# Loops over the image pairs written out with constant waits, no counting step between waits, and the pooled copies ahead of the second norm group's scaling

## The reference, cut to what matters

```python
    x = x + _L0_conv_ref(_gn(x), ...)                 # group norm, then a correlation-driven 7-tap convolution,
                                                      # a 1x5 and a dilated 5x5 depthwise convolution
    t = _to_tokens(x)                                 # 3136 tokens of 64 channels for each image
    t = t + _L1_attn_ref(_ln_t(t), ...)               # linear attention, 16 heads, elu+1 features, cos/sin weights
    t = t + _L1_ffn_ref(_ln_t(t), ...)                # 32 experts: softmax over the tokens, top 8 tokens pooled,
                                                      # two dense layers, results scattered back
    x = _from_tokens(t, x)
```

## Time and profile before

| | |
|---|---|
| median of 3 runs | 3701.57 us (3693.27 to 3703.83) |
| the profiled execution's own time | 3709.65 us |
| its span, first to last instruction | 3707.8 us |
| mean granted TensorE clock | 0.961 |
| instructions in the span | 52162 |
| busy share PE, DVE, ACT, POOL | 86%, 76%, 57%, 41% |

### The profile page before, as it was taken

One profiled execution on the slowest core, in us unless ns is written; L12 is line 12 of the kernel. 1 busy time (PEld: TensorE's weight loads), 2 busy tenths in 40 slices (PEclk: granted clock), 3 DMA queues, 4 the chain that ended last, 5 costly groups with the idle time before them and its releaser, 6 DMA issues.

```text
span 3707.8 us, 52162 instructions
## 1 busy us (share of the span) xinstructions
PE 3197.1 (86%) x16628; PEld 1454.1 (39%) x16628; DVE 2826.8 (76%) x3283; ACT 2119.9 (57%) x2329; POOL 1518.6 (41%) x1078
## 2 busy tenths in 40 slices
PE   3698988988899987989889888998879898898955
PEld 2343335433443334433344334433344333443332
DVE  6887877978778886878778787787878787747843
ACT  1067844777457863678546774468636785445530
POOL 1057611865038631576117651286315762110000
PEclk8799999999999998999989999999999999999977
DMA  1002640045200651026400453006510264104566
GB/s 52 14 4 54 137 110 28 1 104 133 73 19 4 149 131 45 1 48 140 113 28 1 93 131 78 28 1 142 132 47 9 46 140 115 33 0 112 132 166 221
DMA packets 69386, 279.62 MB, mean 75 GB/s; under 512 B 30845, under 2 KB 35485, under 8 KB 64221
## 3 DMA queue, kind: packets, MB, share of 16 engines
q1 hardware_dynamic: 69085, 275.89, 30.6%
HBM read 242.78 MB, written 33.05 MB: 74 GB/s over the span
## 4 chain that ended last, share of the span: by engine, by line
PE 55%; DVE 19%; issue 11%; DMA 7%; ACT 5%; SPq 2%; POOL 1%; DVEq 1%; ACTq 0%; POOLq 0%
PE ps_C L1493 9%; PE ps_D L1560 8%; PE ps_A L1478 5%; PE ps_B L1478 5%; PE ps_D L1493 5%; PE ps_E L1493 5%; DVE region L1132 4%; DMA RB<-r_keep 4%; PE ps_E L1539 4%; DVE region L1123 3%; PE ps_A L1371 3%; DVE arena L948 2%; PE ps_A L1522 2%; DMA r_keep<-RR 2%; PE ps_B L1522 2%
## 5 line engine op out<-in xcount | busy, mean ns | idle before, releaser
L592 POOL TENSOR_TENSOR arena<-arena,UHL 128x896 f32<-128x896 f32 x525 | 1095.2, 2089 | 429.7 <-ACT UHL L724 429.7
L1560 PE MATMUL ps_D<-region,small 128*128 128x448 f32 x1792 | 771.2, 555 | 69.6 <-DVE OS L1159 40.2
L733 ACT ACTIVATE ps_C<-RB 128x896 f32<-128x896 f32 x448 | 410.9, 917 | 308.8 <-DVE region L1132 205.3
L1132 DVE TENSOR_TENSOR region<-region,ps_C 128x896 f32<-128x896 f32 x448 | 484.5, 1081 | 93.1 <-ACT ps_C L733 90.4
L724 ACT ACTIVATE UHL<-arena,W8C 128x896 f32<-128x896 f32 x525 | 542.5, 1033 | 0.0
L570 POOL TENSOR_SCALAR ST<-ST 128x14 f32<-128x14 f32 x64 | 22.5, 352 | 1119.8 <-DVE ST L1003 1118.4
L1560 PEld LDWEIGHTS ps_D<-region,small 128*128 128x128 f32 x1792 | 318.7, 190 | 375.1 <-issue 276.7
L602 POOL TENSOR_TENSOR UA<-region,CS 128x128 f32<-128x128 f32 (+1 forms) x400 | 229.4, 575 | 417.2 <-PE ps_C L1493 368.0
L1493 PE MATMUL ps_C<-region,UA 128*128 128x512 f32 (+1 forms) x800 | 378.3, 595 | 1.9 <-ACT region L658 1.7
L948 DVE SCALAR_TENSOR_TENSOR arena<-arena,W8C 128x448 f32<-128x448 f32 (+1 forms) x243 | 365.1, 1524 | 0.0
L751 ACT ACTIVATE region<-ps_A,NEG 128x1024 f32<-128x1024 f32 (+1 forms) x200 | 222.5, 1113 | 198.4 <-PE ps_A L1478 198.3
(11 more groups left out here) (296 smaller groups left out, 4879.9 us busy)
## 6 DMA issues: line engine op xcount, KB each, us to landing
RB<-r_keep SPq DMA_DIRECT2D x448, 448.0 KB, 5.8
arena<-x SPq DMA_DIRECT2D x8, 1568.0 KB, 7.0
t_keep<-Y SPq DMA_DIRECT2D x7, 1568.0 KB, 5.2
r_keep<-RR SPq DMA_DIRECT2D x448, 7.0 KB, 3.4
w_keep<-region SPq DMA_DIRECT2D x7, 784.0 KB, 5.6
CST<-t_keep SPq DMA_DIRECT2D x2, 1568.0 KB, 10.0
small<-t_keep SPq DMA_DIRECT2D x2, 1568.0 KB, 12.9
plane<-w_keep SPq DMA_DIRECT2D x4, 784.0 KB, 15.8
```

The source lines that it names most:

```text
L592: pool.tensor_tensor(out=X[:, cut], in0=X[:, cut], in1=PRODUCT[m % 3], op=ALU.add).then_inc(pool_taps.sem, 1)
L733: act.activation(here.area(key)[:, :].rearrange("p (c n) -> p c n", c=2)[:, :, 0:PIX], RB[:, cc].rearrange("p (c n) -> p c n", c=2), ACT.C ...
L1132: dve.tensor_tensor(out=q, in0=q, op=ALU.mult, in1=here.area(key)[:, :].rearrange("p (c n) -> p c n", c=2)[:, :, 0:PIX])\
L1560: ins = pe.matmul(here.area(key)[:, 0:PIX], MW[i][:, c, :], Q[s % 3][:, c, :], start=c == 0, stop=c == NCHUNK - 1)
```

## The change

The four loops over the pairs become Python loops, so the body is written out seven times with constants in the waits and addresses (PE, DVE, ACT, POOL and SP each have one). `passed` and its semaphore go, at all of its places. And in DVE's `back` the copies of `pooled` stand ahead of `norm1_scale(pair, 1)`.

```diff
-        def passed(eng):
-
-
-            eng.sem_inc(waits_passed.sem, 1)
-
-
...
                 for s in range(STEPS):
                     sp.wait_ge(*recip_ready.at(pair, s + 1))
-                    passed(sp)
                     for q in range(STRIPS):
...
-            with sp.Fori(0, PAIRS - 1) as pair:
+            for pair in range(PAIRS - 1):
                 pair_of_images(Here("loop", pair))
             pair_of_images(Here("last", PAIRS - 1))
...
                 for w in here.all_emptied([("lg", g) for g in range(NG)]):
                     dve.wait_ge(*w)
-                passed(dve)
                 if here.span == "loop":
                     dve.wait_ge(*pool_taps.at(here.pair + 1, POOL_PIECES))
-                    passed(dve)
...
                 low_part(pair, 0)
-                norm1_scale(pair, 1)
                 if before is not None:
                     pooled(here)
+                norm1_scale(pair, 1)
                 conv_residual(here, pair, 2)
                 conv_residual(here, pair, 3)
...
-            with dve.Fori(0, PAIRS - 1) as pair:
+            for pair in range(PAIRS - 1):
                 links[0] = piece[0] = 0
```

More of the change, by code:

```diff
@@ L377, in program @@
         o_stored = signal("o_stored", unit=16 * STRIPS)
-        waits_passed = signal("waits_passed")
         ones_ready = signal("ones_ready")
@@ L568, in deviations @@
                 pool.wait_ge(*sums.at(pair, g + 1))
-                passed(pool)
                 pool.tensor_scalar(ST[:, g % 2, 2, :], ST[:, g % 2, 1, :], 1.0 / C, LN_EPS, ALU.mult, ALU.add)\
@@ L625, in _ @@
                 deviations(ln1_sums, ln1_std, 0, g, variance.first(g + 1))
-            with pool.Fori(0, PAIRS - 1) as pair:
+            for pair in range(PAIRS - 1):
                 pair_of_images(Here("loop", pair))
@@ L731, in spread_out @@
                 act.wait_ge(*here.room(key))
-                passed(act)
                 act.activation(here.area(key)[:, :].rearrange("p (c n) -> p c n", c=2)[:, :, 0:PIX],
@@ L804, in _ @@
             back(start, 0, False)
-            with act.Fori(0, PAIRS - 1) as pair:
+            for pair in range(PAIRS - 1):
                 pair_of_images(Here("loop", pair))
@@ L1315, in front @@
                     pe.wait_ge(*here.room(key))
-                    passed(pe)
                     for k in range(3):
@@ L1652, in _ @@
             back(start, 0, False)
-            with pe.Fori(0, PAIRS - 1) as pair:
+            for pair in range(PAIRS - 1):
                 pair_of_images(Here("loop", pair))
```

## The result

The changed kernel takes 3653.42 us (median of 4 runs, 3649.62 to 3661.08), the kernel before 3702.70 us (4 runs on the same chip): ratio 0.9865, 95% interval 0.9836 to 0.9894, so 49 us less. The profiled execution took 3652.69 us, 57 us less than the profiled one of before; that one lies 7 us over its kernel's median, so some 8 of the 57 us are the choice of executions.

The account below looks back on a forecast made before the run. PE was taken to bound the K stage, PE and DVE alternately Q, a chain across engines C. Boundaries 17, Q 14 and C 7 us sum to 38 us, giving 3668 us, the middle of 3671.7 and 3663.6; range 3636 to 3691.

Parts of the forecast that it names:

- the likeliest case: Whole kernel: the forecast itself, 3650 to 3680 us, chance 0.57.
- The branch back: Pair boundaries: PE's taken branch delays its first projections; removing it, with the copies moved, gains 17 us.
- my lower bound: Pair boundaries: a gain of 12 us if the third boundary's stall is chance that most runs don't have.
- The pooled copies: DVE at the boundary: moved ahead of the scaling, residual 0.24 us earlier if POOL is late, 0.9 us later if early.
- early POOL: Three of six branches: scaling waits behind the copies, residual 0.9 us later; with the branch gone, 1.3 us gained each.
- Register instructions on DVE: Q stages: short DVE instructions behind waits lose their register steps, 2.0 us a pair, 14 us for seven.
- The C stage: Chain hopping between engines: some ten unhidden register or `passed` steps, 1.0 us a pair, 7 us.
- The K stage: K stages: nothing gained, since PE is busy 143.4 of 146.7 us.
- late fetches: Rival: written-out code is fetched late on PE, block by block, making the kernel slower; chance 0.07.
- The branches for nothing: Rival: branches at 108 ns cost nothing, only the other terms gain, 3683 to 3691 us; chance 0.07.
- The full cost of register steps: Rival: Q stages fall 6 us each to pair 7's length, C 2 us each, 3629 to 3637 us; chance 0.12.
- The branches alone: Rival: register steps are hidden everywhere, only branches gain 12 to 17 us, 3685 to 3693 us; chance 0.17.

Follow-up runs that it names:

- e1: The kernel before with its five loops over the pairs written out, `passed` kept and copies still behind the scaling: 3674.20 us, ratio 0.9927.
- e5: The changed kernel with the copies of `pooled` put back behind the scaling: 3651.59 us, ratio 0.9856 to the kernel before.
- e2: The kernel before with only PE's loop written out: 3685.39 us, ratio 0.9962.
- e7: The kernel before with all loops but PE's written out: 3695.22 us, ratio 0.9985.
- e3: The kernel before with only DVE's loop written out: 3696.47 us, ratio 0.9991.
- e6: The kernel before with only the copies of `pooled` moved ahead of the scaling, loops and `passed` kept: 3684.12 us, ratio 0.9950.
- c1: The changed kernel itself, run once more: 3652.46 us, ratio 0.9857 to the kernel before.
- e8: The changed kernel with six counting steps added at each of two PE waits ahead of the convolution: 3674.65 us, ratio 0.9915 to the kernel before.
- e9: The changed kernel with `passed` kept on PE alone: 3657.66 us, ratio 0.9862 to the kernel before.
- e10: The changed kernel with `passed` kept on SP, POOL, ACT and DVE, none on PE: 3656.24 us, ratio 0.9864 to the kernel before.
- e11: The changed kernel with unread matmuls in PE's gaps, four ahead of the convolution and six at the boundary: 3652.20 us, ratio 0.9858 to the kernel before.

## Why the prediction was right, and where its steps were not

Measured was 49 us by medians, 57 by the profiled executions, for 38 forecast; 3653.4 lies 15 us under the 3668, inside the likeliest case's own range. The total hides a step that was too small, and that it fits so well is in part luck. `passed` stands in my sum with the 0.2 us of a Q stage that it shares with register steps and among the ten steps of a C stage, so with at most 1.2 us a pair, some 8 us. Between e1 and e5, which differ in nothing else, it is worth 22 us. The loops and the copies, with at least 30 of my 38 us, gave 27 (e1), if the move adds nothing to that, as in e5. By its own steps:

**The branch back, 17 us: right, and a little small.** The distances alone were to give 18.8 us (59.6 less seven times 5.83; the copies took off 1.7), and they gave 19.5. Each now has the 2.65 and 3.02 to 3.16 us that pair 7's boundary lent to the sum, as forecast. e2, e7 and the branches' own durations (3.5 to 4.8 us taken, 0.08 us not taken) show that the cause is PE's own branch. By a branch of 108 ns, as the Trainium skill (Advanced Engine Details and Errata, Control Flow Timing) has it, e2 would have given under 1 us, and it gave 15. That a taken branch stalls for its code, as the page Runtime: NRT & Kernel Launch, Instruction fetch mechanics, of the Trainium skill says, agrees with the trace: PE's fetches go from 154 to 135 when its loop alone is written out. The 4 us by which the third boundary stood over the others were most likely chance, as my lower bound had it: nothing like its 12.5 us came back in e3, e6 or e7 (8.8 at most). But e6's two branches of over 5 us show that such long ones do come.

**The pooled copies: one case that did not arise, and one step that was wrong.** The 0.9 us delay for an early POOL did not come in this execution. At all seven boundaries the copies start 1.34 or 1.35 us ahead of the scaling, and DVE still idles 1.04 us for POOL behind them. What I had read as an early POOL was a late PE: ahead of the first boundary its token pooling ran at the 1.2 GHz level in before (granted clock 0.64), and not after (1.00).

```profile
596.74 4.76 PE L1434 MATMUL ps_E<-un,region 128*64 128x128 f32 x49 [1.09 <-ACT region L684]
```

```profile
589.95 3.09 PE L1407 MATMUL ps_E<-un,region 128*64 128x128 f32 x49 [1.11 <-ACT region L668]
```

Where PE is late again, the delay is there as forecast. At e6's first boundary the copies start at 604.60 and hold back the scaling to 604.84 and the residual to 606.07, for 604.94 and 606.26 in my working (this trace runs 0.16 us ahead of before's there):

```profile
604.60 0.34 DVE L1058 COPY PT<-ps_E 64x32 f32 x2 [1.83 <-PE ps_E L1445]
604.84 1.09 DVE L1015 TENSOR_TENSOR region<-region,ST 128x896 f32<-128x896 f32 x1
```

c1 has it at its last boundary. So the three delays in my sum are a matter of the clock from execution to execution, and no fixed price.

And "ps_E comes free earlier in both, but the first projection needs ps_A, so that buys nothing" failed where the loop stands. I followed the wait of the first projection and not that of the instructions ahead of the branch. Alone, the move takes 15.2 us off the boundaries (e6), by covering the very stall that writing out PE's loop removes (e2, 19.4). They are two ways to one gain: together 19.5, and behind straight code the move is worth nothing (e5).

**Register instructions on DVE, 14 us in Q: right in the sum, too large for DVE.** Q gave 15.0 us (18.0 in c1), 2.1 us a pair for the forecast 2.0, and the gaps are 0.034 us as forecast. But I had put 1.8 of the 2.0 us on DVE, 12.6 us in seven pairs. DVE's loop alone takes 9.0 us off Q (e3), all loops but PE's 6.8 (e7), and PE's alone 4.4 (e2). By the medians e3 is only 4 us faster, with an interval from 10 us down to none, so how much of the 9 us reaches the end is not shown. Pair 1's Q of 173.6 stays 4.6 us over pair 7's 169.0: the register instructions were not all of that difference, which speaks for the tap products on ACT.

**The C stage, 7 us: 10.6 us came, and not only by steps.** Routing gave 3.2 and the stretch to residual 2 gave 7.4. In before, undisturbed pairs of that stretch take 31.3 to 32.2 us and after 31.4. The difference lies in pairs that took 34.0 to 35.0, of which before has three and after none (its two disturbed ones take 32.8 and 33.1). The windows of pair 2, whose start of the convolution is slow in before, for that stretch before and after:

```profile
1433.65:1468.65 35.00, 30.14 (x336) 16.86 (x336) 23.70 (x33) 6.60 (x8) 7.97 (x6) 0.89 0.12 24
```

```profile
1420.46:1453.26 32.80, 29.12 (x343) 16.36 (x343) 23.91 (x31) 7.21 (x9) 7.65 (x6) 0.95 0.13 26
```

So most of it is TensorE's clock, which the sum had no term for. e8 shows that more idle ahead of the convolution brings it in every pair; that the steps taken out are what lessened it between before and after is likely from that, but which pair is hit varies from kernel to kernel (e7 has five at 34.8 us). The traces of the kernels without added steps or matmuls sort the same way. The seven with `passed` on PE (before, e1, e2, e3, e6, e7, e9) have two to five pairs each at 34.0 to 35.1 us, whatever became of loops and copies; after, c1, e5 and e10, without it on PE, have none over 33.3. The one thing that sets e9 apart from after is `passed` on PE.

**The K stage, nothing: 3.2 us.** Half a microsecond a pair. It goes with PE's loop, for e2 and e1 have it (855.1, 853.8) and e3, e6 and e7 have about half of it or less (857.0 to 858.5), and at least in part by the clock. In the 6 us behind the ps_B projection the granted clock of pairs 1 to 6 is 0.90, 0.93, 0.69, 0.62, 1.00 and 0.91 in before and 0.93 to 1.00 after: behind a long stall PE runs on at the low level for longer.

**What had no term.** Tail 5.1, head 1.6 and K 3.2 us make half of the 19 us by which the profiled executions' gain passed the sum; the medians' gain passed it by 11. The tail is 489.0 to 493.1 us in the kernels without steps on PE and 494.6 to 496.4 in before, e1, e2 and e9, but 492.3 and 492.7 in e3, e6 and e7, which have them; I did not follow it.

**What stays open.** e1 and e5 differ only in `passed`, and by 22 us. The cuts of the two profiled executions hold 15 of it: to res. 2 6.8 (two of e1's pairs at 35 us, and 0.5 us in the others), Q 4.2, tail 4.0, routing 0.7, head 0.6, less 1 in K. Yet half of the steps alone cost 4 to 5 us by the medians (e9, e10), with the copies in their new place, and those two intervals are wide. I have no run with all steps, straight code and the moved copies, so whether the two halves add up to more than their sum, or whether the place of the copies matters once the steps are there, is not settled. The loops kept with the steps removed were not tried either.

Of the rivals, late fetches are ruled out: pair 1's K, straight code only now, has PE busy 142.93 of 145.90 us, so 2.97 us idle for 3.32 in before, and no stage grew. The "issue" gap ahead of every convolution, 0.82 us in the rows above and the only one of over 0.3 us in pairs 0 to 6, is no late block either; in before the same gap is 1.01 us and ends at DVE's L968. The branches for nothing are ruled out by e2. The full cost of register steps is too: pair 1's Q is 173.6 us, not 170. The branches alone would have ended at 3685, just where e2 stands.

## What to carry to other kernels

PE's branch back costs it a fetch here, 3.3 to 5.2 us, and how much of that reaches the end depends on when the engine gets to the branch. If it waits there for another engine just before, give it that wait earlier: one moved pair of copies (e6) did as much as writing out the loop. Before two edits' gains are added, ask whether they cover the same stall. And a stage's written-out twin in the same trace, here pair 7, is a good yardstick for a boundary, but a poor one for a whole stage that carries less work.

## What the runs showed of the hardware that I had not expected

- A branch back that is taken holds PE for 3.3 to 5.2 us (before, e3, e6, e7); the same instruction not taken is over in 0.08 us.
- A counting step behind a wait costs an idle PE 0.12 to 0.14 us, and by lengthening the idle it cost as much again in the granted clock: 11 + 11 us in e8.
- POOL's power step (L560) takes 3.28 us at the end of `back` in the changed kernel, where DVE's low part (L1011) has started 0.27 us ahead of it. It takes 2.58 us where that part starts 1.24 us ahead (e10) or 0.68 us behind (before, first boundary). That instruction lasts 1.08 to 1.11 us, so in the slow case alone POOL starts while it is under way; that the two get in each other's way is likely from that, and no run tests it.
- Fillers raise the mean granted clock from 0.969 to 0.98 (e11) and gain nothing, since they take longer than the gap they fill: 4.75 us at the boundary, at the full clock.
